# Cross attention's last head pair: who adds one head's weights, and how soon sums, inversions and projection follow

## The reference

```python
x = x + attn(layernorm(x))                       # self attention
h = layernorm(x)
q, k, v = h @ Wq + bq, ctx @ Wk + bk, ctx @ Wv + bv
attn = softmax(q k^T / 8)                        # 16 heads, 2048 x 1601 each
out = (attn v) @ Wo + bo + h
x = x + layernorm(out) * gamma + beta            # cross attention
x = x + fp8_gemm(layernorm(x)) + bias            # the last stage
```

## Time and profile before

| | |
|---|---|
| time of the kernel before, median of 3 executions | 2146.54 us (2145.63 to 2163.06) |
| the profiled execution's own time | 2105.83 us |
| its span, first to last instruction | 2104.0 us |
| outside the span | 1.8 us |
| mean granted clock of PE in it | 0.943 of full speed |
| busy over the span | PE 89%, DVE 65%, ACT 43%, POOL 47% |
| the last pair, blocks 0 to 3, and the tail | from about 1901 us to the end |

### The profile page before, as it was taken

The page is one execution under the profiler, slowest core; times in us unless marked ns, Lnnn a source line. Parts: engine busy times, 40 slices in busy tenths (PEclk is TensorE's granted clock), DMA queues, the critical chain, the costliest instruction groups (busy, mean ns, idle before and its releaser), DMA issues.

```text
span 2104.0 us, 30713 instructions
## 1 busy us (share of the span) xinstructions
PE 1869.7 (89%) x11354; PEld 995.6 (47%) x11354; DVE 1359.7 (65%) x2479; ACT 896.9 (43%) x1794; POOL 982.9 (47%) x808
## 2 busy tenths in 40 slices
PE   7788988889988998899999899999999999898772
PEld 3444444444444544445545455545555545454331
DVE  4667676776722647756746756755765764776888
ACT  2235566666654232333343344343444433344432
POOL 1000000000001445657777777866866876785654
PEclk9769999999989899999999999999999999999986
DMA  4222102240010000000000000000000000000001
GB/s 103 34 33 32 23 11 32 32 83 16 2 50 30 8 1 9 1 1 11 1 1 11 1 1 11 1 1 11 1 1 3 2 1 3 1 5 26 1 21 40
DMA packets 27741, 34.55 MB, mean 16 GB/s; under 512 B 3986, under 2 KB 25811, under 8 KB 25939
## 3 DMA queue, kind: packets, MB, share of 16 engines
q1 hardware_dynamic: 27592, 32.59, 8.6%
HBM read 14.99 MB, written 4.19 MB: 9 GB/s over the span
## 4 chain that ended last, share of the span: by engine, by line
PE 72%; DVE 18%; ACT 5%; issue 3%; SPq 1%; DMA 1%; POOL 1%; ACTq 0%; POOLq 0%; DVEq 0%
PE psum L869 14%; PE psum L884 13%; DVE maxima L1135 8%; PE psum L857 6%; PE psum L777 6%; PE psum L691 5%; PE psum L752 4%; PE psum L873 4%; PE psum L725 4%; ACT weights_room L967 4%; PE psum L907 3%; PE psum L845 3%; DVE parts_room L1223 2%; DVE parts_room L1218 2%; PE psum L789 2%
## 5 line engine op out<-in xcount | busy, mean ns | idle before, releaser
L1135 DVE TENSOR_REDUCE maxima<-psum 128x1 f32<-128x400 f32 (+5 forms) x1664 | 876.4, 581 | 333.8 <-PE psum L857 180.8
L666 POOL TENSOR_TENSOR parts_room<-parts_room,weights_room 128x512 f32<-128x512 f32 (+1 forms) x558 | 708.8, 1301 | 236.1 <-ACT weights_room L1025 233.1
L1025 ACT ACTIVATE weights_room<-psum 128x512 f32<-128x512 f32 (+1 forms) x694 | 369.9, 597 | 519.5 <-PE psum L873 517.5
L967 ACT ACTIVATE weights_room<-psum 128x512 f32<-128x512 f32 (+3 forms) x640 | 297.8, 535 | 226.4 <-PE psum L752 121.5
L1337 POOL TENSOR_SCALAR rstd<-meanvar 128x2 f32<-128x2 f32 (+1 forms) x24 | 7.2, 301 | 693.4 <-DVE meanvar L1085 693.3
L869 PE MATMUL psum<-stack_room,k_hi 64*128 64x512 f32 (+1 forms) x1664 | 309.1, 411 | 14.5 <-ACT weights_room L1025 14.5
L857 PE MATMUL psum<-k_hi,stack_room 64*128 64x400 f32 (+1 forms) x1024 | 261.8, 401 | 53.7 <-DVE maxima L1135 51.4
L857 PEld LDWEIGHTS psum<-k_hi,stack_room 64*128 64x128 f32 x1024 | 147.4, 187 | 225.6 <-issue 115.1
L752 PE MATMUL psum<-stack_room,stack_room 51*128 51x512 f32 (+3 forms) x640 | 194.8, 436 | 43.3 <-ACT weights_room L967 41.6
L869 PEld LDWEIGHTS psum<-stack_room,k_hi 64*128 64x128 f32 (+1 forms) x1664 | 170.2, 184 | 64.8 <-ACT weights_room L1025 28.8
L873 PE MATMUL psum<-shifts,parts_room 64*128 64x512 f32 (+1 forms) x832 | 195.7, 398 | 0.0
(11 more groups left out here) (124 smaller groups left out, 1817.1 us busy)
## 6 DMA issues: line engine op xcount, KB each, us to landing
stack_room<-parts_room SPq DMA_DIRECT2D x96, 128.0 KB
x_block<-x_dram SPq DMA_DIRECT2D x8, 512.0 KB, 4.7
x_middle<-x_block SPq DMA_DIRECT2D x4, 512.0 KB, 3.1
x_block<-x_middle SPq DMA_DIRECT2D x4, 512.0 KB, 5.4
out_dram<-x_block SPq DMA_DIRECT2D x8, 256.0 KB, 2.1
parts_room<-ctx_dram SPq DMA_DIRECT2D x1, 1536.0 KB
stack_room<-shift_rows SPq DMA_DIRECT2D x64, 2.0 KB
parts_room<-wq_dram SPq DMA_DIRECT2D x8, 128.0 KB, 2.2
```

The source lines that it names most:

```text
L666: engine.tensor_tensor(sum_[:kw, :], old[:kw, :], weights[u % NP_WEIGHTS][:kw, :], ALU.add) \
L967: engine.activation(w_self[s % NW][:, m, 0:n], self_scores[(HP * s + m) % SELF_SCORES][:, 0:n], ACT.Exp, scale=SELF_SCALE).then_inc(exp_do ...
L1025: engine.activation(weights[u % NP_WEIGHTS][:kw, :], pair_scores[u % NSCORES][:kw, :], ACT.Exp, scale=CROSS_SCALE).then_inc(pair_exp, 1)
L1135: engine.tensor_reduce(maxima[:, p % 2, i // TB, n, i % TB, ch:ch + 1], bank_of(use + n)[:, 0:real - k0], AX.X, ALU.max) \
```

## The change

Three things change, in the last pair alone. The adds of head 1 are shared out: even pieces (2, 4, ..., 12: six) stay on DVE, odd ones (1, 3, ..., 11: six) go to POOL, behind its own of head 0. As both go into one running sum, each add of head 1 waits for one on the other engine. pair_sums comes at 2 pieces in place of 4, the four inversions and the division come together, at 1, and the projection at 2 in place of 7; so the sums stand two pieces earlier, and the projection, with the whole tail behind it, stands seven pieces (three and a half steps) earlier in the list. The counts that the waits use are now taken from a table made by walking through the stages.

```diff
@@ -211,15 +211,17 @@
             if j == NS - 1:
                 self.put("pair_finish", p, b)
-                self.after(SUMS_LAG, lambda p=p, b=b: self.pair_sums(p, b))
+                self.after(SUMS_LAG if p < NP - 1 else 2, lambda p=p, b=b: self.pair_sums(p, b))
 
     def pair_sums(self, p, b):
         self.put("pair_sums", p, b, banks=1)
+
+        apart = int(p < NP - 1)
         for t in range(TB):
-            self.after(t + 1, lambda t=t: self.put("pair_invert", p, b, t))
-        self.after(TB + 1, lambda: self.put("pair_divide", p, b))
-        self.after(PROJECT_LAG, lambda: self.pair_out(p, b))
+            self.after(apart * t + 1, lambda t=t: self.put("pair_invert", p, b, t))
+        self.after(apart * TB + 1, lambda: self.put("pair_divide", p, b))
+        self.after(PROJECT_LAG if apart else 2, lambda: self.pair_out(p, b))
 
@@ -460,17 +462,9 @@
-    def on_vector(p, m):
-
-        return p == NP - 1 and m == HP - 1
...
+    def on_vector(p, j, m):
+
+        return p == NP - 1 and m == HP - 1 and j % 2 == 0
@@ -502,6 +496,18 @@
+    added_made, made = {}, {True: 0, False: 0}
+    for p, b, j, _ in pair_scores_at:
+        for m in range(HP if j else 0):
+            where = on_vector(p, j, m)
+            made[where] += 1
+            added_made[p, b, j, m] = added_on_vector if where else added_on_pool, made[where]
+
+    def added_with(p, b, j, m):
+
+        return added_made[p, b, max(1, j), m]
@@ -1209,7 +1215,7 @@
                 for m in range(HP):
-                    if j and on_vector(p, m):
+                    if j and on_vector(p, j, m):
                         add(dve, engine, p, b, j, s, m)
@@ -1359,7 +1365,7 @@
                 for m in range(HP):
-                    if j and not on_vector(p, m):
+                    if j and not on_vector(p, j, m):
                         add(pool, engine, p, b, j, s, m)
```

More of the change, by code:

```diff
@@ L461, in pair_last @@
         return HP * (pair_step_of[p, b, NS - 1] + 1)
-    def on_vector(p, m):
-        return p == NP - 1 and m == HP - 1
-    def added_with(p, b, j, m):
-        done = (NS - 1) * pair_finish_no[p, b] + max(1, j)
-        if on_vector(p, m):
-            return added_on_vector, done - (NS - 1) * NB * (NP - 1)
-        alone = (NS - 1) * max(0, pair_finish_no[p, b] - NB * (NP - 1)) + (max(1, j) if p == NP - 1 else 0)
-        return added_on_pool, HP * (done - alone) + alone - (HP - 1 - m if p < NP - 1 else 0)
+    def on_vector(p, j, m):
+        return p == NP - 1 and m == HP - 1 and j % 2 == 0
     consts_set = sem("consts_set")
```

## The result

| | before | after |
|---|---|---|
| median of 20 executions each | 2134.64 us (2104.06 to 2163.06) | 2150.36 us (2127.98 to 2183.83) |
| ratio after to before, with its 95% interval | | 1.0113 (1.0082 to 1.0143) |
| the profiled execution's span | 2104.0 us | 2166.4 us |
| its last stretch, explained below | 204.4 us | 231.3 us |

The account below looks back on a forecast made before the run. A chain through DVE, ACT and PE bounds each block (46.5 us). Block 1 to 1977.7, two loops 109.2, then 12.5 and 28.2 to the end: +23.6 us on 2146.54, 2170.1; range 2142 to 2186.

Parts of the forecast that it names:

- lighter-load rival: Last pair: POOL's load is lighter without DVE's adds beside it; +9.6 us, 2156.1, within 1%; chance 0.20.
- Block 1: From the earlier sums at 1935.0 to the normalisation's end at 1977.7; PE idles 5.8 us before the projection, later some 9.
- The loop: A block's chain through DVE, POOL, ACT and PE from 1977.7: 54.6 us against 46.5 before, run twice (blocks 2 and 3).
- (a): Loop's start: scaling and three exponentials 2.3 us, POOL's two adds of piece 1 2.9, DVE's add of piece 2 1.4: 6.6.
- (f): Loop's end: DVE's add of piece 12 1.4 us, add_norm 5.0, normalisation 0.7: 7.1.
- (b): In the loop: the other half's normalisation 0.7 us, the rounding 5.3, DVE's add of piece 4 1.4: 7.4.
- (d): In the loop: projection 3.4 us, then values, scores and an exponential: 7.0.
- (e): POOL, pieces 6 to 11: nine adds 12.9 us, two L1332 2.7, three rstd 3.7, L1367 1.5, L1373 1.5: 22.3.
- The end: After block 2's first half is normalised at 2086.9: 12.5 us to block 3's projection add, then 28.2 to the span's end.
- DVE's relief wins: Last pair: POOL keeps ahead, DVE stays the bound and loses eight odd adds, 11.1 us: 2135.4; chance 0.12.
- It does nothing: A block's loop stays 46.5 us, shorter reciprocals' wait balancing longer POOL work; within 3 us of 2146.5; chance 0.06.
- Dearer stalls: Scores, values and sums run at the lower clock behind each of five stalls: +40 us, 2186.5; chance 0.10.

Follow-up runs that it names:

- E3: The changed kernel with the whole tail put seven pieces later, behind the early projection: stretch 231.7 us, ratio 1.0143.
- E11: The changed kernel with the projection at its old place, head 1's pieces 1 to 6 on POOL, 7 to 12 on DVE: stretch 217.1 us, ratio 1.0141.
- E7: The changed kernel, projection still early, with head 1's pieces 1 to 6 on POOL and 7 to 12 on DVE: stretch 214.3 us.

## Why the prediction was right

- **The sum.** Forecast +23.6 us and 1.1% slower; measured 1.0113, which is 24 us of 2134.64, and +26.9 us in the stretch (25.8 to the second profile of before). By the medians of all twenty it is 15.7 us, between this forecast and the lighter-load rival's +9.6: the whole time alone would not tell them apart. The stretch and the loop do. The time forecast, 2170.1, stood on a median of three, 2146.54, that twenty executions put at 2134.64; the 2150.36 measured lie inside the range all the same, 20 us below the forecast, and that owes more to the width of the range than to the sum.
- **Block 1.** The projection at 46.1 us from the reciprocal, with PE idle for 5.8: it is at 47.1 and 5.74. The sum has no term for what comes ahead of it: pair 6's last projection came 27.6 us after the reciprocal in place of 26.4. The division in front of that one began no later (25.8 us against 25.7), but took 1.75 us beside POOL where it took 0.68 before. The first scaling was due at 78.1 and came at 79.3, with PE idle for 9.73 where I had some 9, and ACT for 12.28 where I had 9 too.
- **The loop, 54.6 us forecast, 54.9 measured** (2033.33 to 2088.22), but by terms that made up for each other. Steps (a) to (f), forecast and measured from the rows above and their neighbours: 6.6 and 6.5; 7.4 and 8.2; 4.2 and 4.2; 7.0 and 7.8; 22.3 and 21.3; 7.1 and 6.9. In (b) the normalisation cost 2.6 and not 0.7, the add 0.7 and not 1.4. In (d) the block came back to POOL 0.8 us later, of which the projection is 0.4 (3.78 and not 3.4). In (e) the nine adds took 12.2 us where I had 12.9, and L1373 and L1379 1.2 and 1.3 each where I had 1.5.
- **The end.** From the last scaling ahead of block 3's projection to its add I had 12.5 and it took 13.4; from there to the span's end 28.2 and 29.0. DVE's last instruction ends 25.6 us behind this add in both kernels; the 0.8 us lie in the store behind it.
- **Rival "DVE's relief wins"** had its condition tested: it needed POOL less than about 5 us behind. DVE waited 4.84, 7.09 and 7.08 us for POOL at piece 12. It fell. **"POOL's load is lighter"**: the nine adds of step (e) averaged 1.36 us, not 1.28, and the loop took 54.9 us, not the 48.6 that this rival gives. It fell too, though it was right on step (e)'s L1373 and L1379. **"It does nothing"** fell with the loop of 54.9. **"Dearer stalls"** had +40; PE's groups behind a stop took 1.71 and 3.78 us, as the ones of before had (1.66 and 3.78).
- **Wrong in what to look for.** DVE's busy share was to fall from 88% to 75%; from 1986.0 to the end it is 70% (125.7 of 180.4 us by the rows). And E3 showed that I understood the loop less well than its sum says: I took the scaling for the link to cut, but the chain through DVE's queue reforms wherever a tail's part stands ahead of what PE or ACT needs.
- **The rule on shared SBUF access.** The Trainium skill (SBUF — State Buffer, Who interferes with whom) says that only the port pair which DVE shares with GpSimd causes contention, and that it is an exclusive lock. The trace agrees: a DVE instruction that was held waited until 0.1 to 0.2 us before POOL's ended, and POOL's were held in turn (last section). So the prediction was wrong to read the row of adds as a hold shorter than a full block: an add of 1.40 us in it, at 1933.16 of before, began 0.45 us behind POOL's of 1932.71 and was held until 1933.87, and POOL's ended at 1934.01. What was too dear is the price made of it, a whole POOL add of 1.28 us for each; DVE's began inside POOL's, and the holds in these rows are at most 1.1 us. By that price the sum was +34, and the stretch grew by 26.9, nearer to the sum without it (23.6).

Not settled: why sharing by halves gains 17.0 us with the early projection and costs 6.3 with the late one. DVE's first add on its own half waited for POOL for 8.70, 6.22, 8.38 and 11.65 us in the four blocks of E11, and for 8.68, 6.11, 1.32 and 6.21 in E7. These may be the links, but no run took one of them out alone.

## What to carry to other kernels

When each engine issues in a fixed order, work given to a partly idle engine is only cheap if nothing urgent is queued behind the wait that it adds: here 24 adds moved to a POOL busy for 56% of the stretch cost 6.5 to 15.7 us. A product that nobody is waiting for should not be made early: one step of the list for the projection and the tail behind it was worth 15.6 us. And where executions of one kernel differ by 60 us, measure from a fixed instruction to the end in the profile; that repeated to 1.0 us at worst, and told variants apart that the whole time could not.

## What the runs showed of the hardware

Some of DVE's instructions are held when they begin while one of POOL's runs, whatever their own length. In the profile of after these rows of DVE, held and free, are to be set beside those of the same lines shown above:

```profile
1960.91 1.75 DVE L1229 TENSOR_TENSOR parts_room<-parts_room,parts_room 128x512 f32<-128x512 f32 x1
...
2011.29 0.48 DVE L1269 SCALAR_TENSOR_TENSOR x_block<-stack_room,rstd,x_block 128x256 f32<-128x256 f32 x1
...
2020.89 2.63 DVE L1281 TENSOR_SCALAR norm_room<-x_block,meanvar,rstd 128x256 bf16<-128x256 f32 x2
...
2025.81 0.69 DVE L1291 TENSOR_REDUCE norm_room<-norm_room 128x2 f32<-128x512 bf16 x1
2026.53 0.40 DVE L1113 TENSOR_SCALAR norm_room<-norm_room 128x2 f32<-128x2 f32 x1
...
2027.15 1.17 DVE L1117 TENSOR_SCALAR norm_room<-norm_room 128x2 f32<-128x2 f32 x1
...
2028.50 0.69 DVE L672 TENSOR_TENSOR parts_room<-parts_room,weights_room 128x512 f32<-128x512 f32 x1
...
2054.66 0.66 DVE L672 TENSOR_TENSOR parts_room<-parts_room,weights_room 128x512 f32<-128x512 f32 x1
```

And these are POOL's:

```profile
2025.33 1.57 POOL L672 TENSOR_TENSOR parts_room<-parts_room,weights_room 128x512 f32<-128x512 f32 x1 [1.95 <-ACT weights_room L1031]
2027.04 1.26 POOL L672 TENSOR_TENSOR parts_room<-parts_room,parts_room 128x512 f32<-128x512 f32 x1
...
2045.29 1.27 POOL L1338 TENSOR_TENSOR x_block<-x_block,norm_room 128x512 f32<-128x512 f32 x1
...
2054.66 1.81 POOL L1338 TENSOR_TENSOR x_block<-x_block,norm_room 128x512 f32<-128x512 f32 x1
```

L1269 takes 0.48 us here and 1.37 at 2064.39 (+0.9); an add 0.69 here and 1.68 at 2019.29 (+1.0); the two of L1281 2.63 here and 0.70 at 2068.56 (+1.9 for two); and a TENSOR_SCALAR of two elements a partition 1.17, where the line takes 0.17 elsewhere (+1.0). So short instructions lose most by it, for their length.

The hold is no fixed time. It lasts until shortly before POOL's instruction ends. L1117 begins 0.11 us behind POOL's add at 2027.04; with 0.17 us of its own it was held until 2028.15, and POOL's add ended at 2028.30. L1113 takes 0.17 us alone too, but it began 1.20 us into the add at 2025.33: it was held for 0.23 us only, until 2026.76, and that add ended at 2026.90. POOL is held as well: L1338 takes 1.27 us at 2045.29, and 1.81 at 2054.66, where it began together with an add of DVE's that took no more than a free one. Other instructions aren't held: L1291 takes 0.69 us beside POOL's add at 2025.33, and 0.69 alone, and four reciprocals take 3.38 us in either case.

The prediction had priced this for the adds, add_norm and the rounding, but not for the normalisation (2.63 us in place of 0.70) and the division (1.75 in place of 0.69).
